# Loading the first chunk of x in two halves, and the identity and router weights behind chunk 3

## The reference, cut to what matters

```
xn = layernorm(x)                       # mean and variance of each row
s  = gated_linear_recurrence(xn)        # rmsnorm, five projections, scan over time, output projection
g  = silu(moe_top1(xn))                 # softmax router over 4 experts, the best one per token
x  = x + s * g
xn = layernorm(x)
s  = mamba(xn)                          # convolution, selective scan with 16 states x 512 channels
g  = silu(xn @ binarized(weight).T + bias)
out = x + s * g
```

## Time and profile before

| What | Value |
|---|---|
| median of three runs | 1386.43 us |
| the profiled execution's own time | 1387.56 us |
| span of its trace | 1385.7 us |
| busy share PE, DVE, ACT, POOL | 95%, 73%, 63%, 61% |
| last operation that waits for a DMA in the start-up part | `bn_stats` of chunk 2, at 9.49 us |
| first projection matmul (L1691) on the chain | 22.59 us |

### The profile page before, as it was taken

The page is one execution under the profiler, slowest core; times in us unless marked ns, Lnnn a source line. Parts: engine busy times, 40 slices in busy tenths (PEclk is TensorE's granted clock), DMA queues, the critical chain, the costliest instruction groups (busy, mean ns, idle before and its releaser), DMA issues.

```text
span 1385.7 us, 24017 instructions
## 1 busy us (share of the span) xinstructions
PE 1321.7 (95%) x8884; PEld 1066.4 (77%) x8884; DVE 1007.5 (73%) x1358; ACT 877.8 (63%) x1461; POOL 850.3 (61%) x478
## 2 busy tenths in 40 slices
PE   7999999999999999999899999999999999999988
PEld 5544459999999988967668877777778778678777
DVE  7775543332333344478998999999999989989897
ACT  3311121111111131569999999999999999999994
POOL 3132211222222212359989989889989899899994
PEclk9999999999999999999999999999999999999999
DMA  9942136666677655424453553645635554634623
GB/s 299 334 144 99 61 92 249 261 250 247 250 266 264 257 219 188 151 69 88 94 107 77 109 113 77 134 92 104 128 66 125 102 107 94 137 78 96 153 73 77
DMA packets 113188, 205.51 MB, mean 148 GB/s; under 512 B 57647, under 2 KB 84399, under 8 KB 108214
## 3 DMA queue, kind: packets, MB, share of 16 engines
q1 hardware_dynamic: 93814, 146.78, 32.2%
q0 software_dynamic: 19264, 57.26, 19.9%
HBM read 141.81 MB, written 31.00 MB: 125 GB/s over the span
## 4 chain that ended last, share of the span: by engine, by line
PE 54%; ACT 33%; DVE 9%; issue 3%; DMA 1%; POOL 0%; SPq 0%; DVEq 0%; ACTq 0%; POOLq 0%
PE bank L1769 18%; ACT dA L995 14%; ACT dbuT L984 10%; PE bank L1782 9%; PE bank L1691 8%; DVE hst L1594 5%; PE bank L1944 4%; PE bank L1823 2%; PE bank L1952 2%; PE bank L1964 2%; PE bank L1815 2%; PE bank L1834 2%; ACT xpad L927 1%; PE bank L1722 1%; ACT xpad L923 1%
## 5 line engine op out<-in xcount | busy, mean ns | idle before, releaser
L1594 DVE TENSOR_TENSOR_SCAN hst<-dA,carry,bank 128x512 f32<-128x512 f32 x512 | 628.6, 1267 | 33.3 <-PE bank L1944 27.8
L776 POOL TENSOR_TENSOR hst<-hst,c_bc 128x2048 f32<-128x2048 f32 x127 | 549.1, 4418 | 45.5 <-DVE hst L1594 34.8
L995 ACT ACTIVATE dA<-delta,negA 128x512 f32<-128x512 f32 x512 | 354.5, 713 | 0.1
L1944 PE MATMUL bank<-ident,dbuT 128*128 128x128 f32 x2048 | 311.4, 276 | 27.7 <-DVE hst L1594 23.7
L1944 PEld LDWEIGHTS bank<-ident,dbuT 128*128 128x128 f32 x2048 | 239.6, 141 | 126.7 <-DVE hst L1594 60.3
L984 ACT ACTIVATE dbuT<-duT,bT 128x512 f32<-128x512 f32 x386 | 274.5, 712 | 1.5 <-PE bank L1944 1.5
L1769 PEld LDWEIGHTS bank<-f_sb,w_gu 128*128 128x128 f32 x2240 | 256.0, 192 | 4.7 <-issue 2.1
L1769 PE MATMUL bank<-f_sb,w_gu 128*128 128x128 f32 x2240 | 256.9, 275 | 0.7 <-ACT f_sb L853 0.7
L1964 PE MATMUL bank<-ident,hst 128*128 128x128 f32 x1520 | 209.4, 273 | 0.0
L706 POOL TENSOR_TENSOR x_sb<-x_sb,neg_half 128x1 f32<-128x1 f32 x35 | 22.7, 648 | 271.1 <-DVE x_sb L1374 271.1
L1964 PEld LDWEIGHTS bank<-ident,hst 128*128 128x128 f32 x1520 | 174.3, 141 | 0.0
(11 more groups left out here) (228 smaller groups left out, 1659.8 us busy)
## 6 DMA issues: line engine op xcount, KB each, us to landing
w_gu<-in_w_gu SPq DMA_DIRECT2D x35, 2048.0 KB
c_bc<-c_rows SPq DMA_DIRECT2D x64, 512.0 KB, 4.4
hst<-hst POOLq DMA_DIRECT2D x31, 1026.0 KB, 8.8
sorted_x<-w_gu SPq DMA_DIRECT2D x12, 387.0 KB, 11.8
x_sb<-sorted_x SPq DMA_DIRECT2D x35, 129.0 KB
x_sb<-in_x SPq DMA_DIRECT2D x8, 512.0 KB, 8.0
w_d<-in_w_d SPq DMA_DIRECT2D x1, 4096.0 KB, 20.8
x_mix<-x_sb SPq DMA_DIRECT2D x1, 4096.0 KB, 29.9
```

Source lines behind the costliest of these rows:

```text
L776: pool.tensor_tensor(h[:, :, :CH], h[:, :, 1:], c, ALU.mult).then_inc(hc_ready, 1)
L995: act.activation(dA[:, at % DA_BUFS, :], delta[q % B][:, d, :], ACT.Exp, scale=negA[:, d, n:n + 1]).then_inc(dA_ready, 1)
L1594: v.tensor_tensor_scan(h[:, d, 1:], dA[:, at % DA_BUFS, :], bank[4 + u % 2][:], carry1[q % B][:, n, d:d + 1], ALU.mult, ALU.add).then_inc( ...
L1944: ins = pe.transpose(bank[4 + u % 2][:, i * P:(i + 1) * P], dbuT[(DS * q + n) % DBU_BUFS][:, i, d * P:(d + 1) * P], ident[:])
```

## The change

The load of chunk 0 becomes two DMAs of two tiles (256 KB) each. The first half has a new semaphore `ld_half`, the second keeps `ld_x[0]`. The vector engine waits for `ld_half` before tile 0 and for `ld_x[0]` before tile 2; the other chunks are waited for as before. TensorE's first matmuls, which read only tile 0, wait for `ld_half`. The DMAs of `ident` and `w_r` are issued behind chunk 3 rather than behind chunk 1. The sync engine also waits for `ld_half` before it copies `x_sb` to DRAM, much later.

```diff
             for c in range(CHUNKS):
-                sp.dma_start(x_sb[:, c * TPC:(c + 1) * TPC, :],
-                             a["x"][:, c * TPC:(c + 1) * TPC, :]).then_inc(ld_x[c], 16)
-                if c == 1:
+                lo = c * TPC
+                if c == 0:
+                    lo = TPC // 2
+                    sp.dma_start(x_sb[:, 0:lo, :], a["x"][:, 0:lo, :]).then_inc(ld_half, 16)
+                sp.dma_start(x_sb[:, lo:(c + 1) * TPC, :], a["x"][:, lo:(c + 1) * TPC, :]).then_inc(ld_x[c], 16)
+                if c == 3:
                     for t, name in ((ident, "ident"), (w_r, "w_r")):
                         sp.dma_start(t[:], a[name]).then_inc(ld_first, 16)
...
+            sp.wait_ge(ld_half, 16)
             for c in range(CHUNKS):
                 sp.wait_ge(ld_x[c], 16)
...
-                v.wait_ge(ld_x[c], 16)
                 for t in range(c * TPC, (c + 1) * TPC):
+                    if t == 0:
+                        v.wait_ge(ld_half, 16)
+                    elif t == TPC // 2 or t % TPC == 0:
+                        v.wait_ge(ld_x[c], 16)
                     v.bn_stats(st0[:, t:t + 1, :], x_sb[:, t:t + 1, :]).then_inc(tile_stats, 1)
...
-            pe.wait_ge(ld_x[0], 16)
+            pe.wait_ge(ld_half, 16)
             for i in range(WARM):
```

More of the change, by code:

```diff
@@ L347, in build @@
         ld_x = [sem(f"ld_x{c}") for c in range(CHUNKS)]
+        ld_half = sem("ld_half")
         ld_first = sem("ld_first")
```

## The result

The changed kernel takes 1388.85 us, the median of 22 runs (1385.44 to 1391.46), against 1386.39 us before (22 runs): the ratio is 1.0014, interval 1.0008 to 1.002, so about 2 us slower. The forecast was 0.55 us faster, with 1387.9 as the upper end; the time lies outside the range. In size it is under the 0.2% at which the text drew the line, but it is clear of zero, and on the other side. One execution of the kernel before, among those beside e13 and e14, took 4827 us and is left out everywhere.

What follows compares the result with a forecast made beforehand. PE bounds the kernel, busy 95% of the span, with start-up loads on the path. 0.15 us from the half and 0.42 from chunk 2's wait, taken as 0.55, turn 1386.43 into 1385.9 us; range 1383.9 to 1387.9.

Steps and rivals of the forecast that it cites:

- chunk 1's landing: Start-up load: chunk 1, issued 0.47 us later, still lands at 6.0 us, since bytes moved set it, not issue.
- The bounds (5.4 to 6.47): Chunk 1's landing: 5.4 us if free of small packets, gain 1.05 us; 6.47 if tied to issue, gain 0.1 us.
- Chunk 2 failed its forecast: Start-up load: chunk 2 lands at 7.2 to 8.5 us instead of 9.46; later than 9.2 would be wrong.
- the dip of the earlier trace: DMA rate between 5 and 8 us, 262, 176 and 348 GB/s against about 401, laid to ident and w_r passing.
- Rival B: Start-up: the split makes chunk 1 land at 7.2 us, 0.6 us slower, 1387.0; 7 in 100 with milder cases.
- Rival C: Start-up: a longer idle gap before the transposes puts TensorE at 1.2 GHz, 1388.3 to 1392 us; 3 in 100.
- Rival A: Change of layers: shifted work no longer meets the half-clock stretch, 2.65 us less, 1383.2 us; 5 in 100.
- the estimate made from that page: Start-up: if fixed costs of 2.0 us per DMA added up, chunk 1 at 8.0 us, tiles' end 1.9 us late.
- the half lands early: Start-up: first half of chunk 0 lands near 4.2 us instead of 4.82, at the earliest 3.7.
- a wait appears before the fifth tile: VectorE in the start-up: a new wait for chunk 1, 0.3 to 0.6 us, taken as 0.45 us.
- ident and w_r are hidden by the statistics: Before TensorE's transposes: moved loads land by 11.0 us, needed at 13.1, hidden by 2 us of statistics.
- The 0.55 us: Start-up gain carried whole to the end: 0.15 us from the half, 0.42 from chunk 2's wait; between 0.1 and 1.05.

Runs made afterwards that it cites:

- e13: e2 with chunks 0 and 1 loaded as 256 KB (tiles 0 and 1), then 768 KB (tiles 2 to 7): 1388.52 us, 1.0009 of the kernel before.
- e14: e2 with the 2 KB load of cols0 issued between chunk 0 and chunk 1: 1387.33 us, 1.0007 of the kernel before.
- e2: Kernel before with only ident and w_r moved behind chunk 3, chunk 0 whole: 1385.85 us, 0.9995 of the kernel before.
- e12: e2 run again unchanged: 1385.99 us, 0.9995 of the kernel before.
- e1: Kernel before with only chunk 0 in two halves, ident and w_r still behind chunk 1: 1387.98 us, 1.0006 of the kernel before.
- e3: Changed kernel with 14 first matmuls on TensorE instead of 10: 1387.05 us, 1.0004 of the kernel before.
- e6: Changed kernel, but VectorE and TensorE start only when both halves of chunk 0 are in: 1388.69 us, 1.0017 of the kernel before.
- e8: Changed kernel run again unchanged: 1388.71 us, 1.0017 of the kernel before.
- e9: Changed kernel with x laid out chunk by chunk in DRAM, rows 4 KB apart instead of 32 KB: 1388.87 us, 1.0013 of the kernel before.
- e11: e2 with the 2 KB load of cols0 issued first of all: 1386.37 us, 0.9999 of the kernel before.
- e10: e2 with x laid out chunk by chunk in DRAM, rows 4 KB apart instead of 32 KB: 1386.12 us, 0.999 of the kernel before.
- e15: e13 with 14 first matmuls instead of 10: 1387.04 us, 1.0004 of the kernel before.
- e5: Changed kernel with chunk 0 cut by partitions into two DMAs, rows kept at 4 KB, all waiting for both: 1387.34 us, 1.0009 of the kernel before.

## Why the prediction was wrong

- **The step that failed is chunk 1's landing.** The text said: "it is the moving of bytes and not the issue that sets its landing, and I take 6.0." Measured: 8.0 in the profiled execution, 7.0 to 8.1 in all traces with chunk 0 in halves by tiles and another DMA behind. Most bytes were indeed moved: thirteen of sixteen landings of chunk 1 were in by 5.8 us, the last at 8.0. A chunk lands with its slowest engine, and the average rate of all engines, on which the 6.0 was built, can't see that one. The bounds (5.4 to 6.47) were drawn too close for that reason. The earlier trace rows held the hint: chunk 2 came 3.5 us behind chunk 1 for one chunk of bytes. Chunk 2 failed its forecast with it: 9.3 us, where 7.2 to 8.5 was taken and over 9.2 was called wrong.
- **Why the dip, half right.** The forecast laid the dip of the earlier trace rows to the small transfers. Moving them away removes it (e2, e12). But the size of the transfers is not what decides: with a DMA of 256 KB as the further one (changed kernel) a like dip came. A further DMA in second place goes with a late chunk in each trace that has one (changed kernel, e1, e3 to e6, e8, e9, e14); that it is the cause is argued and not shown, as said below.
- **Rival B had the mechanism, not the size.** It put chunk 1 at 7.2 and the loss at 0.6 us, with 7 in 100. At 8.0 the same sum gives 8.03 + 1.42 + 1.50, that is `bn_stats` of chunk 2 at 10.95 on the chain, 1.4 us late, as measured.
- **Rival C had the clock, judged as 3 in 100 because "the gap hardly grows".** It grew from 1.01 to 3.62 us, since chunk 1's delay moved the transposes away while the first matmuls had begun early. B and C are one event: whoever gives B a chance has to price C under B. The text priced C up to 18 us with 2.4 us; the profiled execution lost 1.0 by w0's scaling. Rival A's stretch at the change of layers did shorten in this pair, but by 0.9 us and not by the 2.65 that A priced.
- **The Trainium skill's rule.** The forecast set the Trainium skill's page "DMA: Bandwidth & Descriptors", section "Bandwidth" (batch transfers to 1 MiB or more), against the row in which chunk 1 landed 1.2 us behind chunk 0, and kept the row. The rule pointed to the right side, and the estimate made from that page with a fixed 2.0 us more, chunk 1 at 8.0 us, is the measured number. That is luck: in e11 one DMA more, in first place, made chunk 0 only 0.3 us late. The page's section "Anatomy of one DMA — SWDGE (gpsimd) path" has the 2.0 us from DMAs issued from GpSimd, and these come from the sync engine. Nor is it the size: e13's first load has 256 KB and makes no landing late, and e14's 2 KB cost as much as the half.
- **Right:** the half lands early (3.7 us, where 4.2 was taken; the mean of the text's two rates, 119 and 291 GB/s, gives 1.3 us for 256 KB and an early bound of 3.5, not 1.1 and 3.7, and e1 and e8 had 3.58), a wait appears before the fifth tile (2.88 us, where 0.3 to 0.6 was taken), none before chunk 2, ident and w_r are hidden by the statistics even when late, and the whole lateness of the start reaches the projections.
- **The 0.55 us** was the sum of 0.15 for the half and 0.42 for the move. The move alone has w0's scaling 0.5 us earlier in both traces and a ratio of 0.9995 twice. Its direction is supported by the traces; its time alone can't be told from no change. It is the version to keep: by the ratios (0.9995 against 1.0014) it takes some 2.6 us less than the changed kernel.

What stays open is what holds up the late DMA engines. Ruled out by runs are readers that start before both halves are in (e6), the distance between rows (e9) and the moment of chunk 1's issue alone (e11 issues it at 1.66 too). A further DMA in second place goes with the late chunk, in first place not, each by one trace of 2 KB (e14, e11), and e10 shows a dip with neither. One rival is untested: a further DMA in second place also widens the time between the first issue and chunk 1's, from 0.45 to 0.9 us, while in e11 both move together and in e13 there is no widening. Before the change the late chunk 2 was likewise issued 1.4 us behind chunk 1, and 0.47 us behind it in e2. Whether the DMA or the pause matters, no run tells. Nothing in these traces says what those engines wait for.

## What to carry to other kernels

A load is done when the slowest of its DMA engines is, so a bound on a landing has to come from landings, not from GB/s; and one DMA more, or the pause that it makes, between the first large loads of a program may cost the next one 2 us, as 2 KB did in e14. Matmuls that keep TensorE's clock up have to reach to where the real work begins (e15 against e13), and not only start as early as their data allow. When two rivals share a cause, price them together.

## What was not expected of the hardware

- One engine of sixteen delivers its share of 512 KB 2.2 us after the fifteenth (7.96 against 5.79 us, e14), while the core's engines move 280 to 390 GB/s.
- TensorE's clock was lost after gaps of 3.62 us (changed kernel, e1, e9), 3.61 (e14) and 2.61 (e13), and kept after 2.35 (e8) and 2.44 (e6); in e5 it fell behind a gap of 2.17. The length of the last gap alone does not sort these runs. The changed kernel lost it in one profile (gap 3.62 us) and kept it in another (2.35). The Trainium skill's page "TensorE: Matmul & The Clock Gate", section "HAM oscillation — how this bites in real kernels", has such a fall when TensorE waits between bursts, and the traces agree in that the clock fell behind such waits.
- Rows of 4 KB packed 4 KB apart rather than 32 KB let the first 512 KB land at 4.06 us instead of 4.85 (e10 and e2, one trace of each packed kernel). With the load in halves they did not help: both halves were in at 4.99 us in e9, against 4.28 in the changed kernel.
